# Routing of blocks to experts inside an attention stage: one block at a time, or four blocks together

## The chip, the cores and the metric

The kernel runs on one core of a Trainium2 chip. The metric is the device time of one execution in microseconds (us); lower is better.

## What is computed

The input is x (8192 rows of 128) and a dense adj (8192 x 8192). A graph layer comes first, then a transformer block with causal attention over all 8192 rows (4 heads of 32, 2 key/value heads) and 8 experts, of which each row takes 2.

```python
x = x + _L0_gnn_ref(_layernorm(x, axis=-1), adj, L0_gnn_W)
x = x + _L0_ffn_ref(_layernorm(x, axis=-1)[None], ...)[0]
...
scores = jnp.einsum('bhtd,bhsd->bhts', q, k) / jnp.sqrt(jnp.float32(HD))
...
y = jnp.einsum('bhts,bhsd->bhtd', att, v).transpose(0, 2, 1, 3).reshape(Bx, Tx, Cx)
x = x + y @ wo.T
flat = _rmsnorm(x, ln2_w).reshape(-1, Cx)
probs = jax.nn.softmax(flat @ router_w.T, axis=-1)
tp, ti = jax.lax.top_k(probs, TOPK)
tp = tp / (jnp.sum(tp, axis=-1, keepdims=True) + 1e-09)
```

Each row then goes through its two experts (`w1`, `w3`, `w2`), weighted by `tp`.

## The kernel before, in words

Three stages follow one another: the graph layer, the attention (`attention_stage`), the experts (`expert_stage`). The change is in the attention stage, but for a few tensors whose shape the expert stage shares.

The rows stand in NB = 16 blocks of BT = 512 rows, each block in SUB = 4 tiles of 128. The attention goes through rounds T = 0 to 15, one for each query block. Round T has T + 1 units, one for each key block: v = 0 is the diagonal one. So there are 136 units, numbered through, and `first_unit(T)` is T(T+1)/2. In a unit, TensorE makes scores for four chunks j = 0 to 3 of 128 keys, ScalarE takes their exponential (two ACTIVATEs a chunk, L873, so eight a unit), TensorE weighs the values (L1160) and sums half of the weights (L1170), and GpSimd adds up the other half (`add_chunk`, L758; SUB = 4 buffers of `probs` lie between ScalarE and GpSimd).

Between these matmuls lie GAPS = 16 gaps a unit. In each, TensorE makes scores of the *next* round's queries (`max_pass`, L1130) in one of two PSUM banks `ps_max`, and VectorE takes their maximum (`reduce_tile`, L913). The two banks are a ring: TensorE's use n + 1 waits until VectorE has emptied use n - 1. In round 15 there is no next round and so no maximum.

The routing of an attended block R is threaded through the same gaps, on every engine in its program's order, by hand: `routing(unit)` says which block is at which offset from its start `route_from[R]`. At offset 0 VectorE inverts the denominators (four times 128 columns), divides, and adds the residual to the projection (`project` uses a bank of the ring, as do `turn_block`, `find_logits` and `find_places`). At offset 1 come the mean square, its inverse root (a guess and three Newton steps), the logits; at offset 2 the chances, first and second choice, shares, slots in the experts' lists, and the rows to be sent. At offsets 3 and 4 GpSimd sends the block's rows with eight indirect DMAs (`scatter_rows`, L775), one behind each chunk; each waits for the landing of the one before. The routing's small steps on VectorE go through `then`, where each waits for the one before.

Rounds 1 to 14 carry the routing of blocks 0 to 13 (the early rounds two of them), round 15 that of block 14 (its offset 0 is unit 121), and block 15 is routed behind the last unit with nothing beside it.

## Time and profile before

| what | value |
|---|---|
| median of 3 runs | 4370.78 us (4369.83 to 4376.55) |
| the profiled execution's own time | 4368.3 us |
| its span in the trace | 4366.6 us |
| TensorE / VectorE / GpSimd / ScalarE busy | 3563.8 / 2872.8 / 1618.5 / 1318.8 us |
| attention, first to last exponential | 1488.1 to 3889.0 us |
| the routing of block 15 behind it | to 3921.9 us |

The trace counts from the start of the span. A busy TensorE is not one at its peak, since the ends of matmuls are modelled. PEclk is the share of the full clock (2.4 GHz) that was granted: 1.00 is 2.4 GHz, 0.50 is 1.2 GHz.

### The profile page before, as it was taken

What the parts mean: (1) busy time and instruction counts of PE and PEld (TensorE: products, weight loads), DVE (VectorE), ACT (ScalarE), POOL (GpSimd) and SP (SyncE); (2) the same over time, 40 slices, a digit from 0 to 9 for tenths busy, and PEclk for the clock granted to TensorE, in tenths of its full rate; (3) what the DMA queues carried; (4) which work ended last, traced back from release to release, by engine and by line L of the source; (5) the groups of instructions that cost most, each with busy time, mean ns of one, the idle gap of its engine ahead of it and who ended that gap; (6) DMA issues with size and microseconds to landing.
All of it is one profiled execution on the core that took longest, in us unless ns stands there. A gap on an engine that the chain in (4) does not pass through costs nothing. (4 is left out here: it accounts for less than half of the span.)

```text
span 4366.6 us, 48742 instructions
## 1 busy us (share of the span) xinstructions
PE 3563.8 (82%) x16403; PEld 1339.1 (31%) x16403; DVE 2872.8 (66%) x4390; ACT 1318.8 (30%) x1646; POOL 1618.5 (37%) x1000
## 2 busy tenths in 40 slices
PE   2467899999999588878888898989898989876980
PEld 1333444444444122222222222222222222213540
DVE  7788877334444477778777768777777777215762
ACT  0000000000000133333334344444444445654650
POOL 1000000000000144545455465565656566763661
PEclk8577889999999698888889999999999989988995
DMA  9889988788786265000000000000000000002216
GB/s 378 337 339 346 348 334 316 285 302 298 293 308 235 94 228 206 17 14 15 16 17 6 9 14 5 10 6 9 6 9 6 6 6 6 6 20 76 72 56 192
DMA packets 165285, 572.73 MB, mean 131 GB/s; under 512 B 20193, under 2 KB 55786, under 8 KB 114550
## 3 DMA queue, kind: packets, MB, share of 16 engines
q1 hardware_dynamic: 91304, 457.35, 28.1%
q10 hardware_dynamic: 60432, 88.88, 5.7%
q0 software_dynamic: 13360, 24.03, 1.5%
q8 instruction: 113, 1.85, 0.2%
q14 instruction: 76, 0.62, 0.0%
HBM read 478.22 MB, written 90.57 MB: 130 GB/s over the span
## 5 line engine op out<-in xcount | busy, mean ns | idle before, releaser
L913 DVE TENSOR_REDUCE unit_max<-ps_max 128x1 f32<-128x512 f32 (+3 forms) x2176 | 1354.7, 662 | 485.5 <-PE ps_max L1130 344.5
L758 POOL TENSOR_TENSOR chunk_sum<-chunk_sum,probs 128x1024 f32<-128x1024 f32 (+1 forms) x528 | 1193.6, 2261 | 791.3 <-ACT probs L873 776.2
L873 ACT ACTIVATE probs<-ps_scores 128x1024 f32<-128x1024 f32 (+1 forms) x1088 | 1030.8, 984 | 1030.0 <-PE ps_scores L1149 847.6
L1130 PE MATMUL ps_max<-keep_k_stack,q_stack 96*128 96x512 f16 (+3 forms) x2176 | 819.7, 395 | 253.1 <-DVE unit_max L913 191.9
L1149 PE MATMUL ps_scores<-q_stack,keep_k_stack 97*128 97x512 f16 (+3 forms) x2176 | 662.2, 386 | 22.2 <-ACT probs L873 20.7
L1160 PE MATMUL ps_out<-probs,keep_v 128*32 128x512 f32 (+3 forms) x4352 | 602.7, 628 | 0.6 <-ACT probs L873 0.6
L1130 PEld LDWEIGHTS ps_max<-keep_k_stack,q_stack 96*128 96x128 f16 x2176 | 200.1, 99 | 1224.1 <-DVE unit_max L913 1020.5
L314 DVE TENSOR_TENSOR partial_degree<-partial_degree,ring 128x2048 f32<-128x2048 f32 x240 | 550.0, 2292 | 7.1
L497 PE MATMUL ps_gather<-ring,keep_attended 128*128 128x512 f32 x960 | 449.5, 631 | 22.0 <-DVE keep_attended L338 22.0
L512 PE MATMUL ps_gather_low<-ring,keep_attended 128*128 128x512 f32 x800 | 357.9, 603 | 1.4 <-DVE keep_attended L338 1.4
L277 POOL DMA_DIRECT2D scratch_lower<-lower x15 | 9.3, 619 | 816.3 <-ACT lower L416 816.3
L1170 PE MATMUL ps_sum<-probs,keep_ones_heads 128*32 128x512 f32 (+3 forms) x2176 | 304.2, 627 | 0.0
L1149 PEld LDWEIGHTS ps_scores<-q_stack,keep_k_stack 97*128 97x128 f16 x2176 | 211.5, 101 | 280.0 <-ACT probs L873 96.8
L497 PEld LDWEIGHTS ps_gather<-ring,keep_attended 128*128 128x128 f32 x960 | 193.2, 204 | 263.5 <-issue 263.5
L289 POOL DMA_DIRECT2D keep_k_stack<-k_hi x64 | 31.8, 497 | 562.9 <-DVEq L385 560.9
L1445 POOL DMA_INDIRECT scratch_parts<-moe_y_rows,moe_y_index x156 | 163.9, 1050 | 134.3 <-issue 64.7
L512 PEld LDWEIGHTS ps_gather_low<-ring,keep_attended 128*128 128x128 f32 x800 | 152.4, 194 | 181.8 <-issue 180.3
L481 PE MATMUL ps_gather_low<-ones,partial_degree 128*128 128x1 f32 x512 | 100.5, 330 | 116.8 <-DVEq L333 113.6
L1160 PEld LDWEIGHTS ps_out<-probs,keep_v 128*32 128x32 f32 x4352 | 87.8, 111 | 181.7 <-issue 114.2
L481 PEld LDWEIGHTS ps_gather_low<-ones,partial_degree 128*128 128x128 f32 x512 | 99.1, 301 | 123.6 <-DVEq L333 116.3
L775 POOL DMA_INDIRECT scratch_slots<-keep_rows,keep_slot_index x120 | 118.8, 990 | 41.9 <-DMA scratch_slots<-keep_rows,keep_slot_index 19.7
L460 PE MATMUL ps_turn<-keep_ident,normed 128*128 128x128 f32 x128 | 24.3, 321 | 131.4 <-DVE normed L329 103.8
(223 smaller groups left out, 2853.6 us busy)
## 6 DMA issues: line engine op xcount, KB each, us to landing
ring<-in_adj SPq DMA_DIRECT2D x392, 1024.0 KB, 6.7
scratch_slots<-empty_rows ACTq DMA_DIRECT2D x16, 2080.0 KB, 7.4
scratch_parts<-empty_part ACTq DMA_DIRECT2D x8, 2048.0 KB, 7.7
moe_parts<-scratch_parts SPq DMA_DIRECT2D x64, 256.0 KB, 3.4
moe_x_rows<-scratch_slots SPq DMA_DIRECT2D x39, 260.0 KB
x_in<-in_x SPq DMA_DIRECT2D x16, 256.0 KB, 6.7
x_in<-in_x ACTq DMA_DIRECT2D x16, 256.0 KB, 8.7
cos<-in_cos ACTq DMA_DIRECT2D x16, 256.0 KB, 6.9
```

Source lines behind the costliest of these rows:

```text
L314: add = nc.vector.tensor_tensor(partial_degree[:], partial_degree[:], ring[:, g % R, :], ALU.add)
L481: last = nc.tensor.matmul(ps_degree[:, s:s + 1], partial_degree[:, c * BT + s * P:c * BT + (s + 1) * P], ones[:], start=(c == 0), stop=(c ...
L497: last = nc.tensor.matmul(ps_gather[:], support[:, g * SUB + c, :], ring[:, g % R, c * BT:(c + 1) * BT], start=(g == 0 and c == 0), stop=( ...
L512: last = nc.tensor.matmul(bank[:], support[:, g * SUB + c, :], ring[:, slot, c * BT:(c + 1) * BT], start=(start and c == 0), stop=True, sk ...
L758: nc.gpsimd.tensor_tensor(chunk_sum[:, :, lo:], chunk_sum[:, :, lo:], weights, ALU.add).then_inc(chunk_added, 1)
L873: nc.scalar.activation(probs[:, j, kv, :, lo:], ps_scores[kv][:, :, lo:], ACT.Exp, scale=SCALE).then_inc(exp_done, 1)
L913: nc.vector.tensor_reduce(unit_max[:, i, at:at + 1], bank[:, 0:width], AX_X, ALU.max).then_inc(bank_free, 1)
L1130: last = nc.tensor.matmul(out[:, 0:width], q_stack[0:SHIFT_ROW, T % QBUF, h, s * P:(s + 1) * P], k_stack[0:SHIFT_ROW, h // NREP, G * BT:G ...
L1149: last = nc.tensor.matmul(ps_scores[kv][:, r, lo:], keys, q_stack[:, T % QBUF, kv * NREP + r, lo:], start=True, stop=not diagonal)
L1160: last = nc.tensor.matmul(ps_out[h * HD:(h + 1) * HD, lo:], values[:, G * SUB + j, kv * HD:(kv + 1) * HD], probs[:, j, kv, h % NREP, lo:], ...
L1170: last = nc.tensor.matmul(ps_sum[at * HD:(at + 1) * HD, lo:], keep["ones_heads"][:], probs[:, chunk, 1, r, lo:], start=False, stop=True, s ...
L1445: pool.indirect_dma_start(dram[f"parts{s % CHAINS}"], bass.IndirectOffsetOnAxis(y_index[:, g % 2, s:s + 1], 0), y_rows[:, g % 2, s, :], No ...
```

## The change

Blocks 0 to 14 fall into batches of 0-3, 4-7, 8-11 and 12-14; block 15 is a batch by itself. Each block is still prepared alone (`preparing`: invert, divide, project, add, turn, squares, logits), at a new place: three units from `prepared_at`, which is 8, 10, 12, 14, 25, 27, 29, 37, 48, 56, 67, 79, 92, 106, 121. The new `keep_logits` copies the logits out of the bank. The rest, from `guess_deviation` to `find_slots`, is done once for a batch, on tiles four times as wide (`n` is 16 tiles, 12 for the last batch), and is spread over the gaps from `routed_at` = 17, 40, 82, 124: one step every second gap over 8 units for the first three batches, every gap over 4 units for the fourth. GpSimd sends the rows of a batch from `scattered_at` = 25, 48, 90, 128, one indirect DMA a chunk: 32 in a row, 24 for the fourth. GpSimd instead of VectorE multiplies by the inverted denominators (`divide`). The running count of places, four adds for a block, is now a doubling sum over the batch's tiles (`sum_places`: steps 1, 2, 4, 8, a copy and an add each). There are 49 small VectorE steps a block before; now there are one a block (`keep_logits`) and 56 a batch.

```diff
-    FIRST_ROUTED = 8
-    ROUTE_UNITS = 4
+    BATCH = 4
+    FIRST_PREPARED = 8
     first_unit = lambda T: T * (T + 1) // 2
     units_of = lambda T: [T, *range(T)]
-    ROUTED = NB - 1
-    route_from = []
-    for R in range(ROUTED):
-        route_from.append(max(first_unit(R + 1) + 1, route_from[-1] + ROUTE_UNITS if R else FIRST_ROUTED))
-
-    def routing(unit):
-
-        for R in range(ROUTED):
-            if route_from[R] <= unit < route_from[R] + ROUTE_UNITS + 1:
-                yield R, unit - route_from[R]
+    LAST = NB - 1
+    batches = [range(R, min(R + BATCH, LAST)) for R in range(0, LAST, BATCH)] + [range(LAST, NB)]
+    at_batch = {R: n for Rs in batches for n, R in enumerate(Rs)}
+    prepared_at, routed_at, paces, scattered_at = [], [], [], []
+    for Rs in batches[:-1]:
+        for R in Rs:
+            after = FIRST_PREPARED if not R else prepared_at[-1] + 2 if R > Rs[0] else scattered_at[-1]
+            prepared_at.append(max(first_unit(R + 1) + 1, after))
+        routed_at.append(prepared_at[-1] + 3)
+        paces.append(1 if LAST - 1 in Rs else 2)
+        scattered_at.append(routed_at[-1] + 4 * paces[-1])
+
+    def preparing(unit):
+
+        for R in range(LAST):
+            if prepared_at[R] <= unit < prepared_at[R] + 3:
+                yield R, unit - prepared_at[R]
+    def routing(unit, i):
+
+        for b, start in enumerate(routed_at):
+            gaps, late = divmod((unit - start) * GAPS + i, paces[b])
+            if 0 <= gaps < 4 * GAPS and not late:
+                yield b, divmod(gaps, GAPS)
+
+    def scattering(unit, j):
+
+        for b, start in enumerate(scattered_at):
+            n = (unit - start) * SUB + j
+            if 0 <= n < len(batches[b]) * SUB * TOPK:
+                yield b, n
...
+            def divide(R):
+                pool.wait_ge(inverted, SUB * (R + 1))
+                pool.wait_ge(numerator_copied, R + 1)
+                here = attended[:, R * BT:(R + 1) * BT]
+                nc.gpsimd.tensor_tensor(here, here, denominators[:, R % KEPT], ALU.mult).then_inc(block_divided, 1)
...
+            def scatter_rows(b, n):
+                at, k = n // TOPK, n % TOPK
+                earlier = batches[b][0] * SUB * TOPK + n
+                pool.wait_ge(rows_copied, batches[b][at // SUB] + 1)
+                pool.wait_ge(slots_ready, b + 1)
+                if earlier:
+                    pool.wait_ge(rows_scattered, 16 * earlier)
+                else:
                     pool.wait_ge(slots_emptied, 16 * (SLOT_FILLS + 1))
-                else:
-                    pool.wait_ge(rows_scattered, 16 * (R * SUB * TOPK + n))
-                pool.indirect_dma_start(dram["slots"], bass.IndirectOffsetOnAxis(slot_index[:, s, k:k + 1], 0),
-                                        rows[:, s, k, :], None).then_inc(rows_scattered, 16)
+                pool.indirect_dma_start(dram["slots"], bass.IndirectOffsetOnAxis(slot_index[:, at, k:k + 1], 0),
+                                        rows_of(b)[:, at // SUB, at % SUB, k, :], None).then_inc(rows_scattered, 16)
 
             def route(unit, j):
-                for R, offset in routing(unit):
-                    if (offset, j) == (1, 1):
+                for R, offset in preparing(unit):
+                    if (offset, j) == (0, 3):
+                        divide(R)
+                    if (offset, j) == (2, 0):
                         keep_residual(R)
-                    if offset >= 3:
-                        scatter_rows(R, (offset - 3) * SUB + j)
+                for b, n in scattering(unit, j):
+                    scatter_rows(b, n)
...
+                for i in range(j * SUB, (j + 1) * SUB):
+                    for b, at in routing(unit, i):
+                        if at == (0, 15):
+                            exponentiate(b)
+                for b, n in scattering(unit, j):
+                    if n < len(batches[b]):
+                        copy_rows(batches[b][n])
                 for R in range(NB):
-                    if (unit, j) == ((*route_from, first_unit(NB))[R] - 2, 0):
+                    if (unit, j) == ((*prepared_at, first_unit(NB) - 3)[R], 2):
                         load_block(R)
...
-            def divide(R):
-                dve.wait_ge(inverted, SUB * (R + 1))
-                dve.wait_ge(numerator_copied, R + 1)
-                here = attended[:, R * BT:(R + 1) * BT]
-                nc.vector.tensor_tensor(here, here, denominators[:, R % KEPT], ALU.mult).then_inc(block_divided, 1)
...
+                if R >= BATCH:
+                    earlier = max(E for E in range(R) if at_batch[E] == at_batch[R])
+                    dve.wait_ge(residual_ready, earlier + 1)
+                    dve.wait_ge(rows_ready, earlier + 1)
+                nc.vector.tensor_tensor(x2[:, at_batch[R]], bank[:], z_in[:], ALU.add).then_inc(x2_ready, 1)
...
+            def keep_logits(R):
+                bank = filled_bank()
+                n = at_batch[R] * SUB
+                nc.vector.tensor_copy(logits[:, n:n + SUB], bank[:, 0:SUB * NE].rearrange("p (s e) -> p s e", e=NE)
+                                      ).then_inc(logits_kept, 1)
+                dve.wait_ge(logits_kept, R + 1)
+                dve.sem_inc(bank_free, 1)
...
+            def scale_logits(b):
+                n = len(batches[b]) * SUB
+                here = logits[:, :n]
+                then(nc.vector.tensor_tensor(here, here, over_experts(inv_std2[:, :n]), ALU.mult))
+                then(nc.vector.tensor_reduce(top[:, :n], here, AX_X, ALU.max))
+                nc.vector.tensor_tensor(here, here, over_experts(top[:, :n]), ALU.subtract).then_inc(logits_ready, 1)
...
+            def sum_places(b, steps_taken):
+
+                n = len(batches[b]) * SUB
+                for step in steps_taken:
+                    if step < n:
+                        old, new = (running[(step.bit_length() + m) % 2] for m in (1, 0))
+                        then(nc.vector.tensor_copy(new[:, :step], old[:, :step]))
+                        then(nc.vector.tensor_tensor(new[:, step:n], old[:, step:n], old[:, :n - step], ALU.add))
+            def find_slots(b):
+                n = len(batches[b]) * SUB
+                sums = running[(n - 1).bit_length() % 2]
+                then(nc.vector.tensor_tensor(place[:, :n], place[:, :n], sums[:, :n], ALU.add))
+                then(nc.vector.tensor_tensor(place[:, :n], place[:, :n], taken[:].unsqueeze(1).to_broadcast([P, n, NE]),
+                                             ALU.add))
+                then(nc.vector.tensor_tensor(taken[:], taken[:], sums[:, n - 1], ALU.add))
...
             def route(unit, i):
-                for R, offset in routing(unit):
+                for R, offset in preparing(unit):
                     at = (offset, i)
                     if offset == 0 and i % 3 == 1 and i < 3 * SUB:
                         invert(R, i // 3)
-                    if at == (0, 13):
-                        divide(R)
-                    if at == (0, 15):
+                    if at == (1, 4):
                         add_block(R)
-                    if at == (1, 2):
+                    if at == (1, 12):
                         turn_block(R)
+                    if at == (2, 2):
+                        sum_squares(R)
+                    if at == (2, 6):
+                        keep_logits(R)
+                for b, at in routing(unit, i):
+                    if at == (0, 1):
+                        guess_deviation(b)
+                    if at in ((0, 3), (0, 5), (0, 7)):
+                        refine_deviation(b)
+                    if at == (0, 10):
+                        scale_logits(b)
+                    if at == (1, 1):
+                        find_chances(b)
                     if at == (1, 5):
-                        sum_squares(R)
-                    if at == (1, 6):
-                        guess_deviation()
-                    if at == (1, 7):
-                        invert_deviation(2)
-                    if at == (1, 8):
-                        invert_deviation(1)
+                        choose_first(b)
                     if at == (1, 10):
-                        scale_logits(R)
+                        choose_second(b)
                     if at == (2, 1):
-                        find_chances(R)
-                    if at == (2, 2):
-                        choose(first, best[:, 0, :])
-                    if at == (2, 4):
-                        choose_second()
+                        find_shares(b)
                     if at == (2, 5):
-                        find_shares(R)
-                    if at == (2, 7):
-                        find_slots(R)
+                        count_places(b)
                     if at == (2, 9):
-                        make_rows(R)
+                        sum_places(b, (1, 2))
+                    if at == (2, 13):
+                        sum_places(b, (4, 8))
+                    if at == (3, 1):
+                        find_slots(b)
+                    if at[0] == 3 and at[1] >= 6 and at[1] % 2 == 0 and (at[1] - 6) // 2 < len(batches[b]):
+                        make_rows(batches[b][(at[1] - 6) // 2])
...
             def route(unit, i):
-                for R, offset in routing(unit):
+                for R, offset in preparing(unit):
                     at = (offset, i)
-                    if at == (0, 15):
+                    if at == (1, 4):
                         project(R)
-                    if at == (1, 2):
+                    if at == (1, 12):
                         turn_block(R)
-                    if at == (1, 10):
+                    if at == (2, 6):
                         find_logits(R)
-                    if at == (2, 7):
-                        find_places(R)
+                for b, at in routing(unit, i):
+                    if at == (2, 5):
+                        find_places(b)
```

The order of VectorE's instructions in round 13 of before, at the first and second choice of block 12 (`unit_max` is a maximum of the next round, all else is routing):

```order
L913 TENSOR_REDUCE unit_max<-ps_max 128x1
L995 TENSOR_REDUCE best<-chance 128x4
L996 TENSOR_TENSOR scored<-chance,best 128x32
L997 TENSOR_TENSOR scored<-scored,earlier_first 128x32
L999 TENSOR_REDUCE top<-scored 128x4
L1000 TENSOR_TENSOR first<-scored,top 128x32
L913 TENSOR_REDUCE unit_max<-ps_max 128x1 x2
L1003 SCALAR_TENSOR_TENSOR chance<-first,chance 128x32
L995 TENSOR_REDUCE best<-chance 128x4
```

And of the changed kernel in round 12, at the same steps for blocks 8 to 11:

```order
L958 TENSOR_REDUCE unit_max<-ps_max 128x1 x8
L1049 TENSOR_REDUCE best<-chance 128x16
L1050 TENSOR_TENSOR scored<-chance,best 128x128
L1051 TENSOR_TENSOR scored<-scored,earlier_first 128x128
L1052 TENSOR_REDUCE top<-scored 128x16
L1053 TENSOR_TENSOR first<-scored,top 128x128
L958 TENSOR_REDUCE unit_max<-ps_max 128x1 x10
L1060 SCALAR_TENSOR_TENSOR chance<-first,chance 128x128
L1049 TENSOR_REDUCE best<-chance 128x16
L1050 TENSOR_TENSOR scored<-chance,best 128x128
```

The same five and seven instructions now serve four blocks, on 16 tiles, and ten maxima stand between them in place of two.

GpSimd in round 15 of before, between the diagonal chunks and the first scatters of block 14:

```order
L758 TENSOR_TENSOR chunk_sum<-chunk_sum,probs 128x1024 x6
L764 TENSOR_TENSOR keep_attended<-x,x_in 128x512
L758 TENSOR_TENSOR chunk_sum<-chunk_sum,probs 128x1024 x7
L775 DMA scratch_slots<-keep_rows,keep_slot_index 66048x130
L758 TENSOR_TENSOR chunk_sum<-chunk_sum,probs 128x1024
L775 DMA scratch_slots<-keep_rows,keep_slot_index 66048x130
L758 TENSOR_TENSOR chunk_sum<-chunk_sum,probs 128x1024
```

And of the changed kernel, in the same round:

```order
L786 TENSOR_TENSOR chunk_sum<-chunk_sum,probs 128x1024 x4
L793 TENSOR_TENSOR keep_attended<-keep_attended,denominators 128x512
L786 TENSOR_TENSOR chunk_sum<-chunk_sum,probs 128x1024 x5
L798 TENSOR_TENSOR keep_attended<-x,x_in 128x512
L786 TENSOR_TENSOR chunk_sum<-chunk_sum,probs 128x1024 x20
L810 DMA scratch_slots<-batch_rows,keep_slot_index 66048x130
L786 TENSOR_TENSOR chunk_sum<-chunk_sum,probs 128x1024
L810 DMA scratch_slots<-batch_rows,keep_slot_index 66048x130
```

The division is new on GpSimd, and the scatters begin behind the 29th non-diagonal chunk of the round instead of the 13th; behind these rows 24 scatters stand in turn with chunks, where there were 8.

VectorE behind the last unit of before, in the routing of block 15:

```order
L941 TENSOR_TENSOR keep_attended<-keep_attended,denominators 128x512
L950 TENSOR_TENSOR x<-ps_max,z_in 128x512
L956 TENSOR_SCALAR x2T<-ps_max,ln 128x512
L962 TENSOR_REDUCE square_sum<-squares 128x4
L974 TENSOR_SCALAR square_sum<-square_sum 128x4
L975 TENSOR_SCALAR halved<-square_sum 128x4
```

And of the changed kernel:

```order
L980 RECIPROCAL denominators<-denominators 128x128 x4
L989 TENSOR_TENSOR x<-ps_max,z_in 128x512
L997 TENSOR_SCALAR x2T<-ps_max,ln 128x512
L1004 TENSOR_REDUCE square_sum<-squares 128x4
L1010 COPY logits<-ps_max 128x32
L1018 TENSOR_SCALAR square_sum<-square_sum 128x4
L1019 TENSOR_SCALAR halved<-square_sum 128x4
```

The division has left VectorE, and the logits' copy stands ahead of the mean square's steps; before, the logits were first read behind all of these.

## Rows read from the trace of the kernel before

**Rows 1.** The page: busy time of the engines, share of the span, instructions.
```profile
PE 3563.8 (82%) x16403; PEld 1339.1 (31%) x16403; DVE 2872.8 (66%) x4390; ACT 1318.8 (30%) x1646; POOL 1618.5 (37%) x1000
```

**Rows 2.** Stretches of the attention (windows); columns as in the first row.
```profile
core 0: us, PE busy (x) PEld busy (x) DVE busy (x) ACT busy (x) POOL busy (x), PEclk, DMA share, GB/s
3341.90:3412.80 70.90, 69.47 (x400) 17.86 (x400) 52.13 (x82) 39.26 (x41) 48.29 (x22) 1.00 0.01 2
3230.10:3262.00 31.90, 29.36 (x186) 9.31 (x185) 25.48 (x45) 13.37 (x16) 13.98 (x8) 1.00 0.02 6
3441.10:3464.30 23.20, 20.25 (x113) 5.32 (x114) 15.82 (x28) 9.03 (x11) 10.07 (x5) 0.93 0.06 23
3262.00:3327.80 65.80, 53.05 (x262) 14.55 (x260) 52.19 (x104) 25.04 (x28) 32.09 (x17) 0.87 0.01 4
2011.70:2273.60 261.90, 213.09 (x1115) 60.01 (x1116) 207.41 (x396) 98.70 (x110) 137.35 (x77) 0.89 0.05 16
3282.20:3289.00 6.80, 6.34 (x23) 2.79 (x23) 3.56 (x8) 2.27 (x3) 2.04 (x1) 0.50 0.00 0
3712.70:3889.00 176.30, 162.62 (x1049) 38.74 (x1047) 29.75 (x59) 122.26 (x132) 148.64 (x70) 0.98 0.02 7
3799.10:3879.50 80.40, 78.63 (x508) 17.27 (x496) 0.00 (x0) 62.05 (x65) 75.79 (x33) 1.00 0.03 7
```

**Rows 3.** Timeline of block 12's routing, VectorE: start, duration, instruction.
```profile
3277.39 2.32 DVE L967 TENSOR_TENSOR newton<-inv_std 128x4 f32<-128x4 f32 x1
...
3295.76 1.96 DVE L996 TENSOR_TENSOR scored<-chance,best 128x32 f32<-128x32 f32 x1
```

**Rows 4.** Timeline of the same stretch, TensorE; in brackets its idle time before.
```profile
3281.47 0.39 PE L1130 MATMUL ps_max<-keep_k_stack,q_stack 96*128 96x512 f16 x1 [2.56 <-DVE unit_max L913]
...
3299.18 0.54 PE L1130 MATMUL ps_max<-keep_k_stack,q_stack 96*128 96x512 f16 x1 [2.66 <-DVE unit_max L913]
```

**Rows 5.** VectorE by line, 1600 to 3900 us: count, busy us, mean ns, idle before.
```profile
L967 DVE TENSOR_TENSOR newton<-inv_std 128x4 f32<-128x4 f32 x45 | 30.7, 683 | 0.6
...
L1028 DVE TENSOR_TENSOR scored<-first,place 128x32 f32<-128x32 f32 x15 | 26.0, 1735 | 2.4 <-DVE place L1025 2.4
...
L1033 DVE TENSOR_TENSOR keep_rows<-x,inv_std 128x512 f32<-128x512 f32 x15 | 10.2, 682 | 0.0
...
L986 DVE TENSOR_TENSOR logits<-logits,top 128x32 f32<-128x32 f32 x15 | 2.9, 193 | 0.5
```

**Rows 6.** Timeline of TensorE in the last round, block 14.
```profile
3734.26 1.16 PE L1197 MATMUL ps_max<-wo,keep_attended 128*128 128x128 f32 x8
...
3743.05 1.06 PE L1212 MATMUL ps_max<-router,x2T 128*128 128x8 f32 x8
```

**Rows 7.** Timeline of GpSimd in the last round.
```profile
3788.52 0.98 POOL L775 DMA_INDIRECT scratch_slots<-keep_rows,keep_slot_index  x1 [0.17 <-POOL chunk_sum L758]
...
3796.62 35.02 POOL L758 TENSOR_TENSOR chunk_sum<-chunk_sum,probs 128x1024 f32<-128x1024 f32 x14
```

**Rows 8.** Timeline of ScalarE in the last round.
```profile
3784.92 1.94 ACT L873 ACTIVATE probs<-ps_scores 128x1024 f32<-128x1024 f32 x2 [1.10 <-POOL chunk_sum L758]
...
3799.09 1.94 ACT L873 ACTIVATE probs<-ps_scores 128x1024 f32<-128x1024 f32 x2 [1.60 <-POOL chunk_sum L758]
```

**Rows 9.** Timeline of VectorE in the last round, inside block 14's second choice.
```profile
3755.00 0.19 DVE L995 TENSOR_REDUCE best<-chance 128x4 f32<-128x32 f32 x1
3755.22 2.38 DVE L996 TENSOR_TENSOR scored<-chance,best 128x32 f32<-128x32 f32 x1
```

**Rows 10.** Timeline of all engines behind the last round, block 15.
```profile
3903.05 0.69 DVE L941 TENSOR_TENSOR keep_attended<-keep_attended,denominators 128x512 f32<-128x512 f32 x1
...
3906.74 1.27 POOL L764 TENSOR_TENSOR keep_attended<-x,x_in 128x512 f32<-128x512 f32 x1 [9.87 <-DVE x L950]
...
3908.83 1.84 PE L1212 MATMUL ps_max<-router,x2T 128*128 128x8 f32 x8 [0.94 <-DVEq L958]
...
3909.55 0.17 DVE L974 TENSOR_SCALAR square_sum<-square_sum 128x4 f32<-128x4 f32 x1
...
3912.14 0.19 DVE L982 TENSOR_TENSOR logits<-ps_max,inv_std 128x32 f32<-128x32 f32 x1
```

More of the change, by code:

```diff
@@ L1288, in _ @@
                     turn_max(1)
-            R = NB - 1
-            combine(R)
-            project(R)
-            turn_block(R)
-            find_logits(R)
-            find_places(R)
+            combine(LAST)
+            project(LAST)
+            turn_block(LAST)
+            find_logits(LAST)
+            find_places(len(batches) - 1)
 def expert_stage(nc, NB, dram, keep):
```

245 lines of the change are left out of this document (127 added, 118 removed).

## The prediction

> **What bounds the kernel now.** I read the page first. TensorE is busy 82% of the span, VectorE 66%, GpSimd 37% [rows 1]. A share over stages says little about a change that touches one stage only, so I cut the attention into stretches that begin and end with a unit, and counted units by ScalarE's ACTIVATEs (eight each). The reader is to see how regular it is. A unit without routing, off the diagonal, takes 70.9 / 5 = 14.17 us, with TensorE busy 69.5 of 70.9 us and VectorE 52.1: TensorE is the bound there, and VectorE has 3.8 us a unit to spare, though never more than a gap's worth at a time. The first two units of a round take 31.9 us together, the last one 23.2 [rows 2].
>
> Now the same with routing. From the second routing unit of block 12 on, three units take 65.8 us where 42.5 are due: 23.3 us more, VectorE is busy 52.2 of them, 17.4 a unit in place of 10.4, and the granted clock is 0.87 in place of 1.00. Twelve units of rounds 6 and 7 that hold the routing of blocks 4 to 6 take 261.9 us, where 8 x 14.17 + 31.9 + 2 x 23.2 = 191.7 are due: 70.2, or 23.4 a block [rows 2]. With 0.4 us for the inverts in the unit before (a difference between neighbouring units) and the dearer first blocks, a routed block costs 24 us beside the attention, and blocks 0 to 13 cost 14 x 24 = 336 us.
>
> Why 24, when it is no more work than that? The timeline shows it. VectorE runs a burst of dependent small steps in one gap: two Newton steps are a first one of 2.32 us and five of about 0.2, 3.3 us in all, and TensorE, which has two banks only, then stands 2.56 us for VectorE's maximum; the first choice is 1.96 + 4 x 0.22 = 2.8 us, and TensorE stands 2.66 us [rows 3, 4]. So a burst costs TensorE its length less some 0.6 us. Twice or three times a block the clock then falls to half, 1.2 GHz, for 3 to 7 us: in the stretch from 3282.2 to 3289.0 it is 0.50, right behind the idle 2.56 us, and TensorE's 6.3 busy us there would be half as much at the full clock, so up to 3.2 us are lost [rows 2].
>
> The first step of a burst is long for another reason. The same Newton step takes 683 ns in the mean of 45 (three a block, in two bursts), the slot product 1735 ns (once a block), where a like one takes 193 ns [rows 5]. Per burst that is 3 x 0.5 / 2 = 0.75, 0.75 and 1.5 us of waiting inside the instruction, 1.0 us in the mean of the three, and it never exceeds a GpSimd chunk, 35.02 / 14 = 2.50 us [rows 7]. The row fits a wait for GpSimd's current add, since both read SBUF. The Trainium skill, SBUF — State Buffer, section "Who interferes with whom", states this rule: a VectorE instruction with two SBUF inputs and a GpSimd one that reads SBUF exclude each other for the whole instruction. It speaks against a part of this change, since `scale_logits` now reads both operands from SBUF and the doubling sum adds copies and adds within SBUF; by it each of these can wait once for up to a whole chunk.
>
> **The change, part by part.** (1) Removed: the 336 us of blocks 0 to 13. Everything below is what comes in their place.
>
> (2) Preparation, 14 times. TensorE's matmuls stay: 1.16 for the projection and 1.06 for the logits, eight matmuls each [rows 6], and for the four turns about half of one; these durations overlap the neighbours' a little, so I take 2.5 us of engine time. Four inverts cost 0.4 as before, and each of `add_block`, `turn_block`, `sum_squares` (0.7 us each) is short enough for two banks, with 0.6 us left over for all. 3.5 us a block, 49 us. The bounds are 2.5 (TensorE's time alone) and 6 (every VectorE step beside the maxima paid in full: 3 x 0.7 + 0.2 more). The division leaves VectorE. On GpSimd it takes what the like addition takes, 1.27 us [rows 10], and GpSimd is busy 48.3 of 70.9 us in plain units, so it is covered. `project` waits for it, five gaps later; that cover is some 2 us, and gone it would cost 14 x 1 to 2 us, which lies in the upper bound. The loads of z and x1 go out ten gaps or more ahead of `add_block`, and ScalarE's squares and exponentials no longer stand at the head of its queue before their input exists.
>
> (3) Batches 0 to 2, once each over eight units, in bursts at least four gaps (3.5 us) apart. On 128x128 in place of 128x32 an instruction lengthens by (682 - 193) / 480 = 1.0 ns an element of 96 more, 0.1 us [rows 5], so 0.32 us with its wait; the narrow ones stay at 0.2. Adding 1.0 us of GpSimd wait and taking off the 0.6: guess 0.8 + 0.4 = 1.2; three Newton steps 0.6 + 0.4 each = 3.0; scaling 1.4; chances 1.2; first choice 1.6 + 0.4 = 2.0; second 2.2 + 0.4 = 2.6; shares 1.4 + 0.4 = 1.8; counts nothing but 0.3 for TensorE's matmuls; the sums 1.1 + 0.4 twice = 3.0; slots 2.2 + 0.4 = 2.6; four `make_rows` 0.4. Sum 19.5 us. The clock: only the two or three bursts of 3.2 us are as long as those that brought it down, and they stand alone, so 1.5 drops at 3 us, 4.5. That is 24 us a batch, 72 in all. Bounds: 10 (no GpSimd wait, no drop) and 45 (each burst meets a whole chunk, 12 x 1.3 more, and a drop behind four of them).
>
> (4) The last round. It takes 176.3 us; eight plain units in it take 80.4, 10.05 each [rows 2]. There GpSimd is the bound or level with TensorE: its chunks stand end to end, 14 in 35.02 us, four are 10.0 us. A scatter takes 0.98 us and moves the next chunk by 1.04 [rows 7]; of block 14's eight, five are paid, since from 3784.92 on ScalarE waits for GpSimd, (3799.09 - 3784.92) / 4 = 3.54 us a chunk in place of 2.50 [rows 8]. After: 24 scatters, of which the same three are absorbed, 21 x 1.04 = 21.8; block 14's preparation 2.5; the batch's bursts have no maxima to delay, and its chosen experts are due 21 gaps behind the exponential, which leaves it 13 us for about 11. So 160.8 - 1 (the round's first units are a little short) + 2.5 + 21.8 = 184, or 8 us more. Bounds -3 (scatters absorbed as VectorE's stalls no longer hold GpSimd) and +14 (GpSimd's division and a wait at `find_places` too). In earlier rounds a unit with four scatters needs 4 x 3.54 = 14.16 us of GpSimd, just the 14.17 that TensorE takes, so 96 scatters there are hidden; that cover is thin.
>
> (5) Behind the last unit nothing is covered. GpSimd divides in 1.27 in place of 0.69 us. The logits end at 3908.83 + 1.84 = 3910.7; before, 13 steps from 3909.55 to 3912.1 hid behind that, and now they come after the copy [rows 10]: 1.6 us. The sum of places is longer by some 0.8. 3 us more.
>
> Sum on the profiled execution's own time: 4368.3 - 336 + 49 + 72 + 8 + 3 = 4164 us. That execution is 2.5 us under the median of the runs, so the median would be about 4167; I give 4165.
>
> **The rivals.** *Bursts cost more than by these rows.* If TensorE's stalls do not shrink with spreading, as preparation and batches run near their upper bounds (6 and 40), it is 4368 - 336 + 84 + 120 + 11 = 4247. For it: the round's last units are tight on VectorE, and batch 1 runs through one. Against: single inverts of 0.94 us are almost free today. *Bursts cost less*: 2.5 and 12 a batch give 4368 - 336 + 35 + 36 + 3 = 4106; for it, GpSimd is idle 32% of a plain unit and TensorE may hide more than 0.6 us of a lone burst.
>
> *Slower: GpSimd takes its turn between all steps.* A batch has about 43 steps that read or write two tensors in SBUF. Today only the first of a burst waits. If the wider, longer bursts let a chunk in before each step, 2.2 us a time, a batch costs 95 + 17 = 112, and the sum is 4368 - 336 + 49 + 336 + 11 = 4428. It decides from (336 - 63) / 3 = 91 a batch, 1.7 us a step. For it: in the last round a comparison in the middle of a chain takes 2.38 us, right behind a step of 0.19 [rows 9]. Against: the means of [rows 5], which one wait a burst accounts for. The lock of the Trainium skill's SBUF — State Buffer page would act like this if every instruction had to win it anew against a waiting chunk; the trace's bursts mostly do not.
>
> *No change*: the 24 us belong to the uses of the ring (projection, turn, logits), not to the small steps, so preparation keeps some 18 us; then 4368 - 336 + 252 + 72 + 11 = 4367. Against it stand the two waits of [rows 4], both behind steps that move into the batch.
>
> **How the numbers follow.** Forecast 0.62, costing more 0.16, costing less 0.14, slower 0.05, no change 0.03. A measurement of this kernel tells about 0.2% (9 us) from no change. Faster: 0.62 + 0.16 + 0.14 and a little of the fourth, 0.93; same 0.02; slower 0.05. The forecast's own bounds, not all at one end, are 4130 to 4205. To leave out no more than 2 in 10 the range reaches into both neighbours: 4110 to 4235.
>
> **What would show it.** Right: plain units still 14.17 us; the units with batch steps 16 to 18 us, none over 20; the clock almost always at its full level in rounds 8 to 14; VectorE's busy time down by 200 us or more; GpSimd's chunks and scatters end to end in units 128 to 133, 14.2 us each, and ScalarE waiting for them. Wrong: steps inside a burst that take 1 to 2 us one after another; TensorE waiting for the division at `project`; units with four scatters over 14.5 us in rounds 6, 9 and 12.

## The result, and the profile after

The changed kernel takes 4239.09 us (median of 4 runs, 4228.06 to 4243.45), before 4371.67 (4 runs): a ratio of 0.9691, 95% interval 0.9671 to 0.9712. It is faster by some 133 us, where the forecast was 206 and the range ended at 4235.

The page of the changed kernel, busy times and granted clock in 40 slices:

```profile
PE 3490.7 (82%) x16381; PEld 1324.0 (31%) x16381; DVE 2748.1 (65%) x3882; ACT 1314.1 (31%) x1635; POOL 1639.7 (39%) x1016
...
PEclk8567899999999879999999999999999999978995
```

VectorE is busy 125 us less than in [rows 1], TensorE 73. The windows of the changed kernel, cut at units as in [rows 2] (the columns are in the first row): five plain units of round 14; the three units that prepare block 13; the eight units of batch 0; the eight of batch 2; the last round.

```profile
core 0: us, PE busy (x) PEld busy (x) DVE busy (x) ACT busy (x) POOL busy (x), PEclk, DMA share, GB/s
3449.60:3520.40 70.80, 69.47 (x400) 17.86 (x400) 52.00 (x82) 39.22 (x40) 47.18 (x21) 1.00 0.00 1
3359.00:3407.10 48.10, 45.24 (x265) 13.45 (x264) 38.62 (x62) 24.29 (x26) 30.19 (x14) 1.00 0.04 12
1843.20:2005.60 162.40, 131.60 (x699) 33.22 (x700) 122.72 (x209) 61.65 (x68) 71.69 (x33) 0.89 0.01 3
2946.00:3104.50 158.50, 126.50 (x643) 29.68 (x644) 120.20 (x190) 62.98 (x65) 76.26 (x33) 0.89 0.00 1
3571.20:3762.20 191.00, 164.05 (x1047) 38.46 (x1045) 59.06 (x68) 123.67 (x134) 165.52 (x87) 0.98 0.05 15
```

The reader is to see three things. Plain units are what they were, 70.8 / 5 = 14.16 us. The units that prepare a block take 48.1 us where 15.3 + 2 x 14.17 = 43.6 are due, 4.5 more. And the eight units of batch 2 take 158.5 us where 113.4 are due: 45.1 more, with the clock at 0.89; one by one they take 19.9, 16.8, 15.1, 23.8, 20.9, 19.1, 27.4 and 15.7 us. Batch 0 costs 37.3 and batch 1 26.3 by the same count, 109 us for the three. In a second profile of the same kernel the three cost 37.3, 31.9 and 41.1 us, so a single batch varies by some 5 us from execution to execution. The last round has grown from 176.3 to 191.0 us.

What happens inside batch 2 is plain from its first choice (start, duration, engine and instruction; all engines):

```profile
2996.02 2.36 POOL L786 TENSOR_TENSOR chunk_sum<-chunk_sum,probs 128x1024 f32<-128x1024 f32 x1 [2.77 <-ACT probs L918]
...
2997.72 0.27 DVE L1049 TENSOR_REDUCE best<-chance 128x16 f32<-128x128 f32 x1
...
2998.03 0.51 DVE L1050 TENSOR_TENSOR scored<-chance,best 128x128 f32<-128x128 f32 x1
...
2998.57 0.29 DVE L1051 TENSOR_TENSOR scored<-scored,earlier_first 128x128 f32<-128x128 f32 x1
2998.86 2.34 POOL L786 TENSOR_TENSOR chunk_sum<-chunk_sum,probs 128x1024 f32<-128x1024 f32 x1 [0.48 <-ACT probs L918]
2998.89 0.29 DVE L1052 TENSOR_REDUCE top<-scored 128x16 f32<-128x128 f32 x1
2999.21 2.14 DVE L1053 TENSOR_TENSOR first<-scored,top 128x128 f32<-128x128 f32 x1
...
3002.13 0.10 PEld L1215 LDWEIGHTS ps_max<-keep_k_stack,q_stack 96*128 96x128 f16 x1 [3.95 <-DVE unit_max L958]
3002.13 0.39 PE L1215 MATMUL ps_max<-keep_k_stack,q_stack 96*128 96x512 f16 x1 [3.45 <-DVE unit_max L958]
```

VectorE's burst begins inside a GpSimd add, which ends at 2998.38. GpSimd's adds come in pairs, with some 0.48 us between the two and 1.88 us between two pairs. The burst's first step, a reduction with one input, runs beside the first add without a wait. The second has two inputs in SBUF and waits for the rest of that add (0.51 in place of 0.29 us). The third runs in the pause, the fourth is a reduction again and runs beside the second add, and the fifth, with two inputs in SBUF, takes 2.14 us: it ends just behind that add. The burst is 3.6 us long in place of 1.6, and TensorE stands 3.45 us.

Which instructions wait is the same all through the changed kernel's attention. Of the 191 that are a TENSOR_TENSOR, SCALAR_TENSOR_TENSOR, TENSOR_SCALAR, COPY or CAST within SBUF, 40 take over 1 us, up to 2.87. Of the 68 that read PSUM, and of the 130 reductions and reciprocals of the routing, none does (at most 0.95 us).

### The profile page after: what moved, and what is told of

Same layout as the page of the kernel before. It is cut to its first block and busy times, and to the rows that moved or that the text cites. A ratio compares the mean times of both kernels' runs of the same rounds, so it can differ in the third digit from the quotient of the medians.

```text
span 4241.8 us, 48116 instructions
## 1 busy us (share of the span) xinstructions
PE 3490.7 (82%) x16381; PEld 1324.0 (31%) x16381; DVE 2748.1 (65%) x3882; ACT 1314.1 (31%) x1635; POOL 1639.7 (39%) x1016
## 5 line engine op out<-in xcount | busy, mean ns | idle before, releaser
L1215 PE MATMUL ps_max<-keep_k_stack,q_stack 96*128 96x512 f16 (+3 forms) x2176 | 788.6, 383 | 189.8 <-DVE unit_max L958 126.5
L1234 PE MATMUL ps_scores<-q_stack,keep_k_stack 97*128 97x512 f16 (+3 forms) x2176 | 639.1, 374 | 38.2 <-ACT probs L918 36.6
L1245 PE MATMUL ps_out<-probs,keep_v 128*32 128x512 f32 (+3 forms) x4352 | 580.3, 606 | 0.6 <-ACT probs L918 0.6
L810 POOL DMA_INDIRECT scratch_slots<-batch_rows,keep_slot_index x120 | 118.7, 989 | 40.7 <-POOL chunk_sum L786 18.0
## 6 DMA issues: line engine op xcount, KB each, us to landing
x_in<-in_x ACTq DMA_DIRECT2D x16, 256.0 KB, 11.6
```

Of the source, the lines that this page charges most:

```text
L1215: last = nc.tensor.matmul(out[:, 0:width], q_stack[0:SHIFT_ROW, T % QBUF, h, s * P:(s + 1) * P], k_stack[0:SHIFT_ROW, h // NREP, G * BT:G ...
L1234: last = nc.tensor.matmul(ps_scores[kv][:, r, lo:], keys, q_stack[:, T % QBUF, kv * NREP + r, lo:], start=True, stop=not diagonal)
L1245: last = nc.tensor.matmul(ps_out[h * HD:(h + 1) * HD, lo:], values[:, G * SUB + j, kv * HD:(kv + 1) * HD], probs[:, j, kv, h % NREP, lo:], ...
```

## The experiments

"Excess" below is the time of a batch's eight units over units without routing, from the units' first exponentials. A "burst" is what VectorE does for the routing between two maxima. In the expectations "the port" is the access to SBUF that VectorE and GpSimd are taken to share. All kernels were timed beside runs of the kernel before on the same chip.

### Without GpSimd's adds

In the 24 units of batches 0 to 2 GpSimd adds one column of each weight block; the kernel leaves out the rest of these sums, so its output is not that of the reference.

```diff
+                elif not diagonal and any(start <= unit < start + 8 for start in routed_at[:3]):
+                    pool.wait_ge(chunk_added, unit * SUB + j)
+                    nc.gpsimd.tensor_tensor(chunk_sum[:, :, 0:1], chunk_sum[:, :, 0:1], weights[:, :, 0:1], ALU.add
+                                            ).then_inc(chunk_added, 1)
```

> The changed kernel, but in the 24 units that carry the steps of batches 0 to 2 GpSimd adds one column of each weight block instead of all (the sums of those units are left out). In the changed kernel's trace these 24 units cost 108.8 us over plain ones. Theory A, the port: VectorE's steps wait inside the instruction for GpSimd's adds, which come in pairs, so most bursts meet a second one. Without the adds only the steps' own length is left, and each burst costs it less 0.6 us, 7.5 us a batch: the 24 units cost 20 to 30 us, and the kernel is 75 to 90 us faster than the changed one (about 4155 us). Theory B, length and the two banks: the bursts cost what they do because they are long, wait or no wait; then the units still cost over 80 us and the time stays within 30 us of the changed kernel's 4239.

Measured: 4168.7 us, ratio 0.9533 (0.9516 to 0.9550), 70 us faster than the changed kernel. The window of batch 2's eight units:

```profile
2900.50:3026.40 125.90, 114.68 (x643) 28.86 (x644) 97.64 (x190) 62.84 (x65) 7.92 (x33) 0.99 0.00 1
```

GpSimd is busy 7.9 us there in place of 76.3, the excess is 12.5 us in place of 45.1, and the clock 0.99. No VectorE step of a batch waits (none is longer than the 0.69 us of a row product): its longest burst is 2.3 us, where it was 5.0. The three batches together cost 38 us in place of 109. Theory A stands and B falls, but the kernel gained 70 us and not 75 to 90, and 38 us are more than the 20 to 30 expected. By the ladder further down the lengths of these bursts cost 18 us, and 20 us at half the clock some 10; what the other 10 are stays open.

### The same steps, fitted into GpSimd's pauses, and beside them

```diff
+    ALIGNED = 6
...
+            def route(unit, i):
+                route_once(unit, i)
+                for b, (u, g) in slots(unit, i):
+                    if g == ALIGNED:
+                        slot(b, 2 * u)
+                    if g == ALIGNED + 8:
+                        slot(b, 2 * u + 1)
...
```

`slot(b, k)` is the k-th of 16 bursts: the old steps in the old order, with the choices and the slots cut in two and the row copies paired. In the second kernel ALIGNED is 3.

> The changed kernel with the batch steps of batches 0 to 2 cut into 16 bursts of at most 1.4 us, placed behind gaps 6 and 14 of each of the 8 units, where by the plain units' timeline GpSimd is idle for 1.9 us between two pairs of adds. Theory A, the port: nearly no waits inside instructions; bursts of 0.6 to 1.4 us cost 8 to 12 us a batch instead of 36, and the clock does not fall; 70 to 85 us faster than the changed kernel, about 4160 us. Theory B, length alone: the same total of steps costs the same, less some 0.6 us for each of 4 more bursts; 0 to 15 us faster.

> The same 16 short bursts a batch as in the fitted kernel, but placed behind gaps 3 and 11, where in plain units the second add of a GpSimd pair begins. Theory A, the port and its phase: each burst meets the whole add, some 2 us a burst more, 16 x 2 = 32 us a batch more less what two banks hide; 50 to 100 us slower than the fitted kernel's 4159, so 4210 to 4260, although no burst is longer than in it. Rival C, the cutting alone did it: with bursts of at most 1.4 us the place does not matter, 4150 to 4175.

Measured: fitted 4159.4 us, ratio 0.9505 (0.9484 to 0.9527); unfitted 4286.9 us, ratio 0.9807 (0.9786 to 0.9828). The two kernels differ in one number, and the same bursts on the same tiles, three gaps apart, differ by 128 us. Batch 2 of the fitted kernel:

```profile
2903.50:3022.50 119.00, 113.35 (x642) 28.79 (x642) 96.71 (x188) 62.92 (x65) 76.16 (x33) 1.00 0.00 1
```

Excess 5.6 us, clock 1.00. Batches 0 and 1, which run through the end of a round, cost 11.6 and 9.4, and there the clock was at half for 14 and 10 us. And VectorE in the unfitted kernel's batch 2, the scaling of the logits:

```profile
3019.37 0.28 DVE L1047 TENSOR_TENSOR logits<-logits,inv_std 128x128 f32<-128x128 f32 x1
3019.69 0.29 DVE L1048 TENSOR_REDUCE top<-logits 128x16 f32<-128x128 f32 x1
3020.01 2.41 DVE L1049 TENSOR_TENSOR logits<-logits,top 128x128 f32<-128x128 f32 x1
```

GpSimd's second add stands from 3019.92 to 3022.27. One step runs in the pause ahead of it, the reduction begins there, and the third step takes 2.41 us: a burst of 3.05 in place of 0.9. Ten of batch 2's 16 bursts are over 3 us, 9 and 7 in batches 1 and 0. Its three batches cost 46, 47 and 45 us. Rival C falls: cutting alone makes it worse, since now more bursts meet an add. The unfitted kernel came out slower than its expectation too; its clock was at half for 55, 44 and 31 us of the three batches, which that expectation had not priced.

### How much a burst costs

```diff
...
+                if unit in REDUCES and i == 3:
+                    for n in range(REDUCES[unit]):
+                        then(nc.vector.tensor_reduce(top[:], scored[:], AX_X, ALU.max))
+                if unit in PAIRS and i == PAIRS[unit][0]:
+                    for n in range(PAIRS[unit][1]):
+                        then(nc.vector.tensor_tensor(scored[:], scored[:], first[:], ALU.mult))
```

> The changed kernel with bursts of known length added in plain units, behind gap 3 of each: in units 110 to 118 chains of 1, 2, 3, 4, 6, 8, 10, 12 and 16 reductions of 128x128 within SBUF (one operand; they never waited for GpSimd in any trace here), 0.3 us each; in units 98 to 103 chains of 1, 2 and 4 multiplications with two SBUF operands, behind gap 6 and then behind gap 3. What is read is each unit's time over 14.17 us against the length of its burst. The prediction's rule: length less 0.6 us, at any length. Theory: a short burst is hidden up to some 0.7 us, and a long one costs nearly all of its length, and beyond 2.5 us more than its length, because the clock falls behind it. The multiplications behind gap 6 cost by their own length (0.3 to 1.3 us: under 0.7 us a unit); behind gap 3 each chain has one step of 2 us or more and costs 2 us or more.

Windows of one execution of this kernel, one unit each: with 1, 3, 8, 10 and 16 reductions behind gap 3; then with 2 and with 4 multiplications behind gap 3.

```profile
core 0: us, PE busy (x) PEld busy (x) DVE busy (x) ACT busy (x) POOL busy (x), PEclk, DMA share, GB/s
3427.20:3441.30 14.10, 13.89 (x80) 3.58 (x80) 10.59 (x18) 7.82 (x8) 9.38 (x5) 1.00 0.01 2
3455.50:3469.90 14.40, 13.96 (x80) 3.57 (x80) 11.19 (x21) 7.88 (x9) 9.49 (x5) 1.00 0.00 0
3499.90:3515.80 15.90, 13.96 (x80) 3.57 (x80) 12.51 (x25) 7.80 (x8) 9.37 (x5) 1.00 0.00 0
3515.80:3534.00 18.20, 15.58 (x80) 3.86 (x80) 13.20 (x27) 7.95 (x8) 10.06 (x5) 0.91 0.00 1
3552.70:3572.80 20.10, 15.54 (x80) 3.80 (x80) 14.89 (x34) 7.85 (x8) 9.49 (x5) 0.92 0.01 1
3291.70:3305.90 14.20, 13.89 (x80) 3.57 (x80) 10.99 (x20) 7.88 (x9) 9.48 (x5) 1.00 0.01 2
3305.90:3325.70 19.80, 16.98 (x80) 3.95 (x80) 13.70 (x21) 7.92 (x9) 10.01 (x5) 0.83 0.00 0
```

| burst, us | 0.28 | 0.60 | 0.92 | 1.24 | 1.88 | 2.52 | 3.16 | 3.81 | 5.09 |
|---|---|---|---|---|---|---|---|---|---|
| unit over 14.17 us | 0.0 | 0.0 | 0.2 | 0.5 | 1.15 | 1.8 | 4.05 | 4.5 | 5.9 |

From 0.92 to 2.52 us a burst costs its length less 0.73: the prediction's rule, and nearly its constant. From 3.16 us on 1.4 to 1.6 us come on top, and in each of these units the clock is at 1.2 GHz for 3.4 us; TensorE had stood 2.37 us ahead of the first such fall, and 1.73 us in the unit before, where the clock stayed. The last window shows the port: four multiplications, 1.25 us of work, crossed an add and became 3.37 us, the unit cost 5.7 us more and the clock was at half for 6.8 us. Behind gap 6 the same chains of 1, 2 and 4 cost 0.0, 0.0 and 0.7 us. Of the expectation one part fell: one and two multiplications behind gap 3 slip into the pause and cost nothing; only the chain of four met the add.

### Batches of one block, plain and fitted

```diff
-    BATCH = 4
+    BATCH = 1
...
-        paces.append(1 if LAST - 1 in Rs else 2)
+        paces.append(1)
```

> The changed kernel with batches of one block (BATCH = 1), each spread over four units at one step a gap: the spacing is kept, the batching undone. Theory A, the number of bursts counts: 14 blocks with some 30 us of steps each beside 4.4 us of preparation, 14 x 34 = 480 us in place of 336, so the kernel is at or above the time of before, 4370 to 4500 us. Theory B, spacing is what helps: a block costs 10 us or less, and the time stays near the changed kernel's, 4220 to 4290 us.

The fitted one has ten bursts behind gaps 6 and 14 of five units:

> Batches of one block, as in the kernel with BATCH = 1, but with the steps cut into ten bursts of at most 1.7 us, placed behind gaps 6 and 14 of five units. Theory A, the port and its phase: a burst costs some 0.5 us, so a block costs 5 to 9 us beside 4.4 us of preparation, 14 x 11 = 154 us in place of the 338 of before and the 466 of BATCH = 1 unfitted; with a last round of some 170 us this gives 4185 to 4225 us, faster than the changed kernel although nothing is batched. Rival: it takes the batching, since 14 x 10 bursts cost as many stalls; 4370 us or more.

Measured: one block 4510.6 us, ratio 1.0322 (1.0295 to 1.0349); fitted one block 4219.8 us, ratio 0.9642 (0.9625 to 0.9658). Spread out but not batched, a block's steps cost 29.6 us (units of block 12) beside the preparation, and the kernel is 3% slower than before, a little beyond theory A's 4370 to 4500: spacing alone buys nothing. Fitted into the pauses, they cost 5.3 us a block (block 9, whose units meet no end of a round), as theory A had it, and the kernel without any batching is some 19 us faster than the changed one.

### The division and the running count

> The changed kernel with the division back on VectorE, at gap 13 of the first preparing unit. Theory A, the port: the division takes 1.8 us with its wait on VectorE and costs TensorE some 1.2 us a block beside the maxima; 14 x 1.2 less 1 us behind the last unit gives 10 to 20 us slower than the changed kernel, about 4254 us. Rival: it was hidden on VectorE too, and within 5 us of 4239.

```diff
...
-                nc.gpsimd.tensor_tensor(here, here, denominators[:, R % KEPT], ALU.mult).then_inc(block_divided, 1)
...
+                nc.vector.tensor_tensor(here, here, denominators[:, R % KEPT], ALU.mult).then_inc(block_divided, 1)
```

> The changed kernel with the running count over the batch's tiles (15 adds of 128x8, 7 in the first place and 8 in the second) in place of the doubling sum's 8 copies and adds. By the trace one narrow add and its wait take 0.2 us: 3.0 us in place of 2.2 us a batch, and the two bursts grow from 1.1 to some 1.5 us; 2 to 8 us slower than the changed kernel's 4239. Rival: a copy within SBUF waits for GpSimd as much as an add does, so fewer steps of either kind change nothing, within 4 us.

```diff
...
-                        then(nc.vector.tensor_copy(new[:, :step], old[:, :step]))
-                        then(nc.vector.tensor_tensor(new[:, step:n], old[:, step:n], old[:, :n - step], ALU.add))
...
+                        then(nc.vector.tensor_tensor(running[0][:, tile], running[0][:, tile], running[0][:, tile - 1],
+                                                     ALU.add))
```

Measured: 4251.5 us with the division back on VectorE, ratio 0.9721 (0.9704 to 0.9739); 4244.3 us with the running count, ratio 0.9708 (0.9680 to 0.9736). Both intervals overlap the changed kernel's. In the traces the attention is 6.6 and 1.9 us longer than in the changed kernel's first profile, but 3.2 longer and 1.5 shorter than in its second. The division's place costs 0.2 us a block in the units of preparation, where theory A had 1.2: its number of 4254 us came, its mechanism did not. Most of the 6.6 us lie in batch 1, which differs by 5.6 us between two profiles of the changed kernel itself. So GpSimd's division is worth some 3 us by itself, what the rest of the 12 us between the medians is stays open, and the doubling sum is worth nothing that these runs can tell.

### Fewer scatters in the last round

```diff
-    batches = [range(R, min(R + BATCH, LAST)) for R in range(0, LAST, BATCH)] + [range(LAST, NB)]
+    batches = [range(R, min(R + BATCH, LAST)) for R in range(0, 12, BATCH)] + [
+        range(12, 14), range(14, LAST), range(LAST, NB)]
```

> The fitted kernel with blocks 12 and 13 as a batch of their own, routed from unit 109 and scattered from 117, so that the last round carries block 14's steps and 8 scatters alone. Theory: GpSimd is the bound in the last round, 16 scatters x 1.04 us less there, which takes it from 191 to 174 to 178 us, while the fifth batch costs 6 to 10 us in round 14: 5 to 11 us faster than the fitted kernel, about 4151. Rival: the scatters in unit 120 (diagonal) or the additional batch give it all back, within 3 us.

Measured: 4149.8 us, ratio 0.9495 (0.9472 to 0.9518). The last round takes 177.0 us in place of 191.1, as expected, and round 14 with the fifth batch 2.5 us more, where 6 to 10 were expected; the attention is 11.9 us shorter. The medians, of two chips, are 10 us apart, and the two intervals overlap.

### The graph layer

The changed kernel's first exponential came at 1505.9 us, 17.8 later than before, in a stage that the change does not edit. It resizes kept tensors, though: `slot_index` and `taken` together are 32 bytes a partition smaller, and all that is allocated behind them stands 32 bytes lower.

```diff
-                         ("slot_index", [P, 4 * SUB, TOPK], mybir.dt.uint32), ("taken", [P, NE], F32)))
+                         ("slot_index", [P, 4 * SUB, TOPK], mybir.dt.uint32), ("taken", [P, NE], F32), ("padding", [P, 8], F32)))
```

> The changed kernel with a tensor of 32 bytes a partition behind the kept ones, so that what the graph layer allocates stands at the same places as in the kernel before. In the changed kernel's trace the first exponential comes 17.8 us later than before, at an unchanged graph layer. If the places cause it, the first exponential is back at 1488 us and the median falls by 10 us or more, to 4228 or less; if it is variation from execution to execution, the time stays at 4239 within 6 us.

> The kernel before, unchanged, for one more profile of its graph layer and its expert stage. In its first profile the first exponential came at 1488.1 us and 477.6 us lay behind the last; in nine of the changed kernel and its variants they are 1497 to 1506 and 480 to 490. If this is variation between executions, the profile shows 1495 us or more here; if it belongs to the change, 1488 again.

> The changed kernel as it is, as the measure for the padded one on the same chip. If places in SBUF cost the graph layer 10 us or more, it is 10 to 15 us slower than the padded kernel here; if not, the two are within 5 us of each other. The first exponential of its profile: 1505 us if the first profile was typical, below 1500 if it varies.

> The changed kernel with 32 bytes a partition behind the kept tensors, so that the graph layer's tensors stand where they stood before. On another chip it had 4224.9 us against the changed kernel's 4239.1. Places cause it: 10 to 15 us faster than the changed kernel on this chip too. Variation or the chip: within 5 us.

> The fitted kernel with blocks 12 and 13 as a batch of their own, and the same padding. If the padding gains, it is 10 us faster than without it, 4140 us; if not, it is at 4150 us within 6.

Measured: 4224.9 us with the padding, ratio 0.9666 (0.9638 to 0.9693), and, on another chip, 4226.6 beside 4237.5 without it; ratios 0.9662 (0.9647 to 0.9677) and 0.9682 (0.9668 to 0.9696). The first exponentials: 1496.2 in the second profile of before, 1497.8 and 1492.9 with the padding, 1500.1 in the second of the changed kernel; 4144.7 us for the split kernel with padding, 0.9468 (0.9455 to 0.9481), where it had 4149.8 without, its first exponential at 1503.1. So the first exponential alone varies by some 8 us within one kernel. The padded kernel was 11 to 14 us under the unpadded twice, but the intervals overlap, and the third pair gained 5 us with a later first exponential. In the profiles of the first two pairs only 7 to 8 us lie ahead of the first exponential; 9 lie in the attention, where batches and early rounds vary from execution to execution. So a loss from the shift is not shown.

## Why the prediction was wrong in size

The direction, the engine that bounds the attention and the cause of the old cost were right; the sum was 80 us too low on the profiled execution. Its steps:

| step | forecast | measured |
|---|---|---|
| blocks 0 to 13 removed | -336 | -338 |
| (2) preparation, 14 times | +49 | +72 |
| (3) batches 0 to 2 | +72 | +109 |
| (4) last round | +8 | +15 |
| (5) behind the attention | +3 | +2 |
| start of the attention | 0 | +18 |
| not assigned | 0 | -3 |
| sum | -204 | -125 |

A part of the 18 us at the start of the attention is variation: in the second profiles of the two kernels it differs by 3.9 us (1496.2 and 1500.1).

**(3) is the step that failed**, "1.5 drops at 3 us" and "1.0 us of GpSimd wait" for every burst alike. The rule by which I turned a burst's length into TensorE's idle time holds: the ladder gives 0.73 us hidden where I took 0.6. But the waits are not 1.0 us each. Against the kernel without the adds, where a batch's bursts sum to 18, 18 and 17.3 us, they sum to 35.1, 30.1 and 39.7: 17, 12 and 22 us of waits, where I had 12. And they are bunched: eight or more of 17 bursts are nearly free, and 6, 4 and 8 bursts are over 3 us, since a step that meets the beginning of an add waits for all of it. A mean over the old bursts hid this. By the ladder's rule the lengths cost 22.6, 17.6 and 27.9 us; that leaves 14.7, 8.7 and 17.2 us of the excess. The clock was at half for 34, 17 and 34 us, and half of these times, 17, 9 and 17 us, is an estimate of what that costs. So of the 37 us that (3) missed, by this estimate some 10 lie in the lengths of the bursts and 27 in the clock, which I had at 4.5 a batch. I had taken long bursts that stand alone to be nearly harmless for the clock; the ladder shows one burst of 3.16 us enough. (In the fitted and the unfitted kernel, and in the one without the adds, the same count misses a batch's excess by up to 9 us, so the split is a rough one.)

**(2)** was mis-sized: 4.4 us a block in the late rounds (0.4, 1.8 and 2.2 in the three units) where I took 3.5, and some 6 for the first four blocks and 5.5 for the next three, whose preparations overlap and which meet the rounds' ends.

**(4)**: the scatters did what they were to do. GpSimd is end to end, a chunk and a scatter take 3.54 us, ScalarE waits 1.61 us each time. What was missed stands ahead of them. From 3607.28 GpSimd has seven adds end to end, 17.39 us, and there VectorE makes two steps an add. VectorE's timeline of the changed kernel in the last round:

```profile
3609.70 0.17 DVE L1019 TENSOR_SCALAR halved<-square_sum 128x12 int32<-128x12 int32 x1
3609.91 2.26 DVE L1021 TENSOR_SCALAR guess<-halved 128x12 int32<-128x12 int32 x1
3612.20 0.17 DVE L1022 COPY inv_std<-guess 128x12 f32<-128x12 f32 x1
3612.41 2.26 DVE L1027 TENSOR_TENSOR newton<-inv_std 128x12 f32<-128x12 f32 x1
```

From `square_sum` (3609.38) to the last rows the 59 instructions of this chain take 55 us, 18 of them over 2 us each; in the kernel before it was 25 us with five. My slower rival was this mechanism, and here it is real. The rows came late, and ScalarE, first in its queue with the copy of them, held up the exponentials:

```profile
3663.15 0.62 ACT L893 COPY batch_rows<-batch_rows 128x512 f32<-128x512 f32 x1 [4.70 <-DVE batch_rows L1109]
```

That made unit 128 take 15.7 us in place of 10; eight scatters were absorbed by it, not three. Late in the round GpSimd lost another 3.4 us in two places:

```profile
3726.87 0.99 POOL L810 DMA_INDIRECT scratch_slots<-batch_rows,keep_slot_index  x1 [2.48 <-issue]
...
3735.04 0.98 POOL L810 DMA_INDIRECT scratch_slots<-batch_rows,keep_slot_index  x1 [1.24 <-DMA scratch_slots<-batch_rows,keep_slot_index]
```

**(5)** held: the routing of block 15 takes 2.4 us more. For blocks 0 to 14 `project` never waits for the division.

Of the signs, plain units at 14.17 us came, and so did scatters in rounds 7, 9 and 13 that cost nothing (14.17 us a unit where no preparation shares it). Batch units of 16 to 18 us, a clock almost always full and VectorE down by 200 us did not; steps of 1 to 2 us one after another, the sign of being wrong, came in the last round.

Of the rivals, "bursts cost more than by these rows" came closest, 4247, with the mechanism named nearly right and a chance of 0.16. In part that is luck: its terms for preparation and batches, 84 and 120, were above the measured 72 and 109, and a later start of the attention that no term held made up for it. The Trainium skill, SBUF — State Buffer, section "Who interferes with whom", calls the pair of SBUF ports that VectorE and GpSimd share an exclusive lock. The trace agrees: steps of 0.2 to 0.3 us take 2.1 to 2.5 us, beside a whole add of 2.36. I had weighed that rule as a price of one mean wait a burst; taken with the adds' places in the unit, it would have told which bursts pay.

## What to carry to other kernels

Before pricing small VectorE steps beside GpSimd work that reads SBUF, draw both on one time axis over a period of the loop, and find the pauses. A chain that fits a pause costs its length less what the buffers hide, here 0.73 us: four multiplications cost 0.7 us there and 5.7 us three gaps earlier, where they met an add. Fitting gained 80 us here, more than half of what batching and all the rest did. And price a stall by what it does to the clock too: in the ladder two bursts of 1.88 us cost 2.3 us together, one of 3.81 us cost 4.5.

## What the hardware showed beyond expectation

A single stall can bring the granted clock down. In the ladder a burst of 2.52 us left it at 1.00, one of 3.16 us, with TensorE idle for 2.37 us, brought it to 1.2 GHz for 3.4 us, and the unit's excess jumped from 1.8 to 4.05 us. The length of the burst does not decide it alone: in the changed kernel's batch 2 a burst of 3.11 us (at 2975.2, TensorE idle 1.47 us) left the clock at full, and in the kernel without GpSimd's adds one of 2.32 us (at 3001.2, TensorE idle 2.01 us) brought it down for 3.4 us. What it hangs on beyond TensorE's idle time these runs do not settle. And with GpSimd never pausing, VectorE's dependent steps within SBUF, the plain copy and TENSOR_SCALAR among them, advance two an add, some 2.5 us, though each is 0.17 us of work.
